# Masked attention over 200 items per user: where a block's context is projected, and how the mask is loaded

## What is computed

```python
def reference(target_key, item_keys, item_values, mask, W_target, W_item, W_value):
    B, L, D = (512, 200, 64)                     # users, items, features; all float32
    q = target_key @ W_target.T
    k = einsum('bld,ed->ble', item_keys, W_item)
    v = einsum('bld,ed->ble', item_values, W_value)
    scores = einsum('bd,bld->bl', q, k) / sqrt(D)
    scores = scores - 1e8 * (1 - mask)           # mask is int32, 0 or 1
    w = softmax(scores, axis=1)
    return einsum('bl,bld->bd', w, v)
```

## Time and profile before

| | |
|---|---|
| median of three runs | 133.96 us (133.62 to 134.03) |
| the profiled execution's own time | 133.99 us |
| its span, first to last instruction | 132.2 us |
| TensorE matmul busy | 72.5 us, 55% of the span |
| VectorE, ScalarE, GpSimd busy | 19.6, 7.8, 5.3 us |
| read from HBM | 53.07 MB, mean 402 GB/s over the span |
| mean granted TensorE clock | 0.815 of full |

### The profile page before, as it was taken

How to read it: one execution, slowest core, us unless ns; L and a number is a source line. 1 busy time by engine, 2 the same in 40 slices (tenths; PEclk the granted TensorE clock), 3 DMA queues, 4 the chain that set the end, 5 groups by cost and what they waited for, 6 DMA issues and landing times.

```text
span 132.2 us, 1303 instructions
## 1 busy us (share of the span) xinstructions
PE 72.5 (55%) x536; PEld 22.7 (17%) x536; DVE 19.6 (15%) x55; ACT 7.8 (6%) x26; POOL 5.3 (4%) x18
## 2 busy tenths in 40 slices
PE   0000007992499214992089522993069839949981
PEld 0000003331122011221012111231011122302250
DVE  6000002004200500005100310004200130033060
ACT  3000001003000000003000010002000000011000
POOL 7400000000000000001000000001000000001000
PEclk9999999998569955599559995589658975797698
DMA  8699799799979997999899889979998989999900
GB/s 272 272 544 510 306 520 434 310 496 496 434 310 485 496 434 326 482 498 389 373 480 496 372 387 481 498 327 420 398 472 387 480 387 455 403 443 406 393 18 10
DMA packets 2450, 53.22 MB, mean 402 GB/s; under 512 B 784, under 2 KB 784, under 8 KB 1040
## 3 DMA queue, kind: packets, MB, share of 16 engines
q1 hardware_dynamic: 1872, 53.07, 93.5%
q10 hardware_dynamic: 576, 0.13, 0.5%
HBM read 53.07 MB, written 0.13 MB: 402 GB/s over the span
## 4 chain that ended last, share of the span: by engine, by line
DMA 57%; PE 25%; issue 12%; DVE 3%; ACT 1%; POOLq 0%; SPq 0%; DVEq 0%; ACTq 0%
DMA value<-values 57%; PE ps_context L457 7%; PE ps_scores L438 6%; PE ps_context L466 4%; PE ps_context L460 3%; PE ps_context L474 3%; PE ps_small L485 1%; DVE context L381 1%; DVE context_slots L377 1%; ACT expd L263 0%; DVE biased L341 0%; DVE second_biased L338 0%; DVE neg_max L344 0%; SPq L185 0%; POOLq L74 0%
## 5 line engine op out<-in xcount | busy, mean ns | idle before, releaser
L438 PE MATMUL ps_scores<-first_tile,sta_query 128*32 128x400 f32 x256 | 30.9, 651 | 9.0 <-DMA first_tile<-keys 8.4
L457 PE MATMUL ps_context<-value,sta_full 128*32 128x512 f32 x64 | 13.5, 989 | 10.8 <-DMA value<-values 10.8
L438 PEld LDWEIGHTS ps_scores<-first_tile,sta_query 128*32 128x32 f32 x256 | 9.6, 138 | 28.5 <-issue 19.6
L417 PE MATMUL ps_small<-first_tile 64*64 64x128 f32 x4 | 0.7, 444 | 19.9 <-DMA first_tile<-first 19.9
L377 DVE TENSOR_TENSOR context_slots<-ps_context,in_octet 128x512 f32<-128x512 f32 x4 | 2.8, 692 | 38.0 <-PE ps_context L474 32.5
L338 DVE SCALAR_TENSOR_TENSOR second_biased<-ps_scores,in_pair,mask_bias 128x200 f32<-128x200 f32 x4 | 1.7, 426 | 43.6 <-PE ps_scores L438 43.6
L466 PE MATMUL ps_context<-value,sta_half 128*32 128x512 f32 x64 | 7.7, 598 | 0.0
L239 POOL COPY half_twice<-expd 128x128 f32<-128x128 f32 x4 | 1.4, 345 | 113.2 <-ACT expd L263 113.2
L444 PE MATMUL ps_turn_full<-ident,expd 128*128 128x128 f32 x4 | 1.3, 328 | 8.2 <-ACT expd L263 8.2
L474 PE MATMUL ps_context<-value,sta_full 128*32 128x512 f32 x48 | 5.7, 592 | 0.0
L460 PE MATMUL ps_context<-value,sta_eighth 128*128 128x512 f32 x8 | 5.5, 775 | 0.0
(11 more groups left out here) (48 smaller groups left out, 34.5 us busy)
## 6 DMA issues: line engine op xcount, KB each, us to landing
value<-values SPq DMA_DIRECT2D x3, 6400.0 KB, 23.0
first_tile<-keys SPq DMA_DIRECT2D x2, 6400.0 KB, 22.0
first_tile<-first SPq DMA_DIRECT2D x1, 7024.0 KB, 19.0
first_tile<-keys SPq DMA_DIRECT2D x2, 3200.0 KB, 18.2
value<-values SPq DMA_DIRECT2D x1, 2304.0 KB, 12.4
value<-values SPq DMA_DIRECT2D x1, 2048.0 KB, 16.8
value<-values SPq DMA_DIRECT2D x1, 1280.0 KB, 19.4
value<-values SPq DMA_DIRECT2D x1, 512.0 KB, 20.2
```

Of the source, the lines that this page charges most:

```text
L438: last = nc.tensor.matmul(ps_scores[g * GU:(g + 1) * GU, 0:QB], window(sta_query, g, k), key[:, c:c + QB], start=k == 0, stop=k == QUADS - 1)
L457: nc.tensor.matmul(ps_context[g * GU:(g + 1) * GU, :], window(sta_full, g, k), value[:, c:c + OB], start=k == 0, stop=False)
```

## The change

TensorE turns and projects the context of block n-1 after the scores of block n, ahead of turning the weights of block n. A register of TensorE holds the count that the waits use. ScalarE's order follows: it copies the turned context of n-1 ahead of the exponentials of n, and finishes n-1 after it has placed the weights of n. The transpose of the last block waits in addition until the result of block 2 has been written.

The mask leaves the first transfer and becomes a tensor of its own, in three transfers of 88, 32 and 8 rows of 3200 bytes, which SyncE issues between the first transfer and values 0. VectorE waits for all three ahead of the mask bias.

```diff
--- before.py
+++ after.py
@@ -41,7 +41,7 @@
 ROUND = 16
 
 
-def masked_attention_kernel(nc, first, keys, values, out):
+def masked_attention_kernel(nc, first, mask_rows, keys, values, out):
 
     B, D = out.shape
     L = FULL + HALF + EIGHTH
@@ -56,8 +56,9 @@
     W_ITEM = W_TARGET + D
     TARGETS = W_ITEM + D
     W_VALUE = TARGETS + B // 2
-    MASK = W_VALUE + D
-    FIRST = MASK + NBLK * L
+    FIRST = W_VALUE + D
+
+    MASK_ENDS = (88, 120, P)
     assert tuple(first.shape) == (P, FIRST)
     assert 2 * D == P and B == 4 * P
 
@@ -86,8 +87,8 @@
         w_target = first_tile[:, W_TARGET:W_ITEM]
         w_item = first_tile[:, W_ITEM:TARGETS]
         targets = first_tile[:, TARGETS:W_VALUE]
-        w_value_twice = first_tile[:, W_VALUE:MASK]
-        mask = first_tile[:, MASK:FIRST].bitcast(mybir.dt.int32)
+        w_value_twice = first_tile[:, W_VALUE:FIRST]
+        mask = sb("mask", [P, NBLK * L], mybir.dt.int32)
         value = sb("value", [P, V_COLS])
 
         w_both = sb("w_both", [P, 2 * D])
@@ -153,6 +154,7 @@
         s_both_copied = sem("s_both_copied")
         s_query = sem("s_query")
         s_sta_query = sem("s_sta_query")
+        s_mask = sem("s_mask")
         s_mask_bias = sem("s_mask_bias")
         s_second = sem("s_second")
         s_biased = sem("s_biased")
@@ -183,6 +185,10 @@
             for n in range(NBLK):
                 if n == 0:
                     sp.dma_start(first_tile[:], first).then_inc(s_key, 16)
+                    begin = 0
+                    for end in MASK_ENDS:
+                        sp.dma_start(mask[begin:end, :], mask_rows[begin:end, :]).then_inc(s_mask, 16)
+                        begin = end
                 elif n < NBLK - 1:
                     sp.wait_ge(s_key_used, n)
                     sp.dma_start(key, keys[n - 1]).then_inc(s_key, 16)
@@ -291,15 +297,17 @@
                 act.dma_start(out_blocks[n], result[:, n, :]).then_inc(s_stored, 16)
 
             place_odd_queries(0)
-            for n in range(NBLK - 1):
+            for n in range(NBLK):
+                if n > 0:
+                    copy_context_t(n - 1)
                 exponentials(n)
                 place_full(n)
-                place_odd_queries(n + 1)
-                copy_context_t(n)
-                finish(n)
-            exponentials(NBLK - 1)
-            place_full(NBLK - 1)
-            place_late_full()
+                if n == NBLK - 1:
+                    place_late_full()
+                if n > 0:
+                    finish(n - 1)
+                if n < NBLK - 1:
+                    place_odd_queries(n + 1)
             finish(NBLK - 1)
             act.wait_ge(s_stored, 16 * NBLK)
 
@@ -396,8 +404,9 @@
                                         ALU.mult).then_inc(s_context_t_copied, ROUND)
 
             place_even_queries(0)
-            dve.wait_ge(s_key, 16)
-            nc.vector.tensor_scalar(mask_bias[:].rearrange("p n l -> p (n l)"), mask, -1.0, MASKED, ALU.add, ALU.mult).then_inc(s_mask_bias, 1)
+            dve.wait_ge(s_mask, 16 * len(MASK_ENDS))
+            nc.vector.tensor_scalar(mask_bias[:].rearrange("p n l -> p (n l)"), mask[:], -1.0, MASKED, ALU.add,
+                                    ALU.mult).then_inc(s_mask_bias, 1)
             for n in range(NBLK):
                 shift(n)
                 repeat_eighth(n)
@@ -500,20 +509,27 @@
 
             def turn_context_late():
                 pe.wait_ge(s_context_late, 1)
+                pe.wait_ge(s_result, NBLK - 1)
                 nc.tensor.transpose(ps_context_t, context_late[:].rearrange("p e d -> p (e d)"), ident[:]) \
                     .then_inc(s_context_t, 1)
 
 
 
+
+            before_register = pe.alloc_register("before")
+            pe.reg_mov(before_register, 0)
             with nc.Fori(ROUND, ROUND * (NBLK + 1), ROUND, engines=[mybir.EngineType.PE]) as done:
                 score(done)
+                with pe.If(done > ROUND):
+                    before = pe.snap(before_register)
+                    turn_context(before)
+                    project(before, D)
                 turn_weights(done)
                 weigh_first(done)
                 with pe.If(done < ROUND * NBLK):
                     weigh_halves(False)
                     weigh_second()
-                    turn_context(done)
-                    project(done, D)
+                pe.reg_add(before_register, before_register, ROUND)
             weigh_late()
             turn_context_late()
             project(ROUND * NBLK, P)
@@ -549,10 +565,10 @@
         np.concatenate([inputs["L0_rec_W_target"], inputs["L0_rec_W_item"], half_targets,
                         np.asarray(inputs["L0_rec_W_value"]).T], axis=1) for half_targets in halves], axis=0)
     mask_rows = np.ascontiguousarray(mask.reshape(NBLK, P, L).transpose(1, 0, 2).reshape(P, NBLK * L))
-    small = np.concatenate([small, mask_rows.view(np.float32)], axis=1)
 
     arrays = {
         "first": np.concatenate([k[0], small], axis=1),
+        "mask_rows": mask_rows,
         "keys": k[1:],
         "values": np.concatenate([full[:, 0], eighth, half[:, 0], half[:, 1], second], axis=2),
     }
```

## The result

The changed kernel takes 137.00 us (median of six runs, 135.90 to 137.73) against 133.67 us for the kernel before on the same chip (median of six, 133.42 to 134.03). The ratio is 1.0235, with a 95% interval of 1.0206 to 1.0265. The prediction was 132.9 us, in a range from 132.6 to 134.0.

A forecast was written before the change was run, and what follows sets the result against it. Loads were taken as the floor, TensorE's chain 0.5 us apart. The contexts' add moves from 128.42 to 127.15 (-1.25), the tail costs 0.2: net -1.05 from 133.96, so 132.9 us, range 132.6 to 134.0.

The forecast's parts named there:

- The mask: Mask transfers ahead of values 0: same bytes, only the rows' deal to engines could matter, bounds -1.0 to +0.4 us.
- The 1.0 us by which the first transfer was to land earlier: First transfer without 8 mask rows per engine: block 0's scores start 1.0 us earlier, weighing still waits for values 0.
- The relief of the late engine: Last loads: late engine among five with fewer mask rows, last landing 126.65 instead of 127.4; chance put at a half.
- The projection moved: Block 3 on TensorE: scores start 3.8 us earlier, little arrives; halves end at 123.2 to 124.9, ahead of the loads.
- The frame: Whole kernel: load queue never runs dry; TensorE's order alone gains at most 0.5 us, more needs earlier last loads.
- a clock that rises half way: Second half of block 3's scores: between 2.8 us (full clock) and 5.5 (half), scores ending at 116.3 or 115.6.
- rival C: Last block at low clock, idle stretch amid its scores: +0.8, 134.7 us; decides if scores end behind 117.2; chance 0.06.
- the cover of the projection: Between block 3's scores and weighing: block 2's transpose and projection, 1.5 us, fit into 2.9 us, some 2 idle.
- the copy's place on ScalarE: Copy ahead of the exponential: ready about 0.4 us after the scores, the exponential's input not before 1.4.
- the 2.9 us from scores to weighing: TensorE in block 3: weighing starts 2.9 us after the scores end, as before the change.
- no loss in blocks 1 and 2 from the order: Scores of blocks 1 and 2 wait for their keys, not the projection, so nothing changes there.
- 0.5 us from the last piece to the add: End of the loads: late matmuls 0.24 us, with first entry's latency and hand-over 0.5, then VectorE adds the contexts.

The follow-up runs named there:

- keys_rows64: Kernel before, with the second half of keys 3 loaded as two transfers, rows 0 to 63 and 64 to 127: 145.93 us in one run.

## Why the prediction was wrong

**The mask, the step that failed.** The prediction asked only how the rows are dealt to the *engines*, and put the bounds at -1.0 and +0.4 us on that. The deal fits what was assumed (packets 2035). But it priced a mask row at an engine's ordinary rate, 0.125 us, whatever the other engines do. Transfers of blocks of neighbouring rows made a mask row cost 215 ns in the median instead of 126, and the first packets of values 0, which ran beside them, up to 3.4 us instead of 1.89; all 16 engines together fell to 320 GB/s. That several engines then share an entrance to SBUF is the rule of the Trainium skill named above; for the 88 rows it stays an argument, since no run shows which rows an engine gets. Measured: 2.1 to 2.2 us by the medians (1.0154 for the mask alone, 1.0235 against 1.0068 for its shape), +2.4 us on values 0 and on the loads behind by the profile, 3.0 in the run with the mask alone; 0.1 us with one transfer of 128 rows, 0.4 with three by columns, 0.2 with even and odd rows. The packet records account for 1.5 us of it; the rest, engines that end at different times, was not taken apart. The trace of before shows 128 rows as the only shape, so its rate was no bound for another shape, and the cost needed a bound above it. Half the rate for the mask's own 8 rows per engine would have made that bound +1.0 us, still under half of what was measured, because the load behind is slowed as well. The 1.0 us by which the first transfer was to land earlier did not show either: it landed 0.6 later, and with one mask transfer of 128 rows only 0.2 earlier (19.68), within the scatter of single profiles.

**The relief of the late engine** did not show. The last piece landed at 129.7, not 126.65, and two engines instead of one lagged.

**The projection moved, right in mechanism, wrong in size.** The frame held: the queue never ran dry, the order could gain 0.5 us at most. The scores started right behind the weighing of block 2 (107.29, where before 3.8 us lay between), stopped for the keys, and went on at half clock. The prediction took a clock that rises half way through the second half, 4.2 us; it took 5.39, near the bound of 5.5. So the scores end 5.6 us behind the keys' landing and not 4.2, and TensorE's chain stays the last: 131.41 for the add is the halves' end (127.52 + 1.92 = 129.44) plus 1.97, the 1.95 of the prediction. Its own rival C named this mechanism and this point of decision, at a chance of 0.06. Measured alone it is +0.4%, 0.5 us, where C had +0.8.

**What held:** the cover of the projection (it runs from 120.00 to 121.1, the weights are turned at 122.12), the copy's place on ScalarE, the 2.9 us from scores to weighing (120.07 to 122.96), no loss in blocks 1 and 2 from the order, and 0.5 us from the last piece to the add where the loads set the end.

**The sum as measured:** in the two profiles loads +2.4, TensorE behind them +0.6 us, together the 3.0 by which the add (131.41 - 128.42) and the span (135.2 - 132.2) moved. The medians give 2.2 for the mask's shape and 0.9 for the rest, together 3.1 (1.0235).

## What to carry to other kernels

A load is priced by the rows it covers, not only by its bytes or by how many engines take part: load all 128 partitions at a time, or if a transfer must cover some of them, take every second one and not a block of neighbours. A slow transfer also slows the load behind it for as long as both run. Work moved off the head of a stage is worth only what the next wait leaves of it; here it moved TensorE's idle time into the middle of the scores, where it cost the clock as well. And where a trace shows only one shape of transfer, its rate is no bound for another shape.

## What the runs showed of the hardware

- 64 neighbouring rows per transfer move 200 to 205 GB/s with all 16 engines shown as busy, against 397 to 410 for 128 rows (one run, `keys_rows64`); a busy DMA share does not say that the rate is full.
- While transfers of 88, 32 and 8 neighbouring rows ran, 16 packets of the next load, which covers all 128 rows, took 2.0 to 3.4 us instead of 1.89.
- 64 even or odd rows per transfer move what 128 rows do (499 against 498 GB/s in the same window, 126 ns for the median row in both).
- The packet count of transfers of 88, 32 and 8 rows (35 ends) fits 11, 16 and 8 engines, and the 8-row one of another run has eight ends.
- Five extra matmuls whose result nobody reads made the 32 score entries behind them take 2.89 us instead of 5.39, at no cost to the end.
- A program that fetched 16 KB of instructions near its end had a span 1.2 us longer than one that did not, with its last add 0.2 us earlier. One profile each, and the first was one of its program's longer executions.
